# Two-layer cross-attention on one core: scores computed twice, the second time transposed

## The reference

```python
# layer 0: 8 heads of 40; the last 4 context rows are kept apart as "ca"
query, keyt, valt = x @ Wq, enc @ Wk, enc @ Wv              # enc: 371 rows
hs = mha(query, keyt, valt)
ca_q1 = einsum('btc,th->bch', ca, Wq_ca)[:, indices, :]
ca_hs1 = mha(ca_q1, x, x)                                   # the second attention
ca_hs2 = mha(ca_hs1 @ Wq, ca @ Wk_ca, ca @ Wv_ca)           # the third, over 4 keys
x1 = (hs + ca_hs2) @ Wout + b_out + x
# layer 1: 20 heads of 16, over all 375 rows
out = mha(x1 @ Wq, ctx @ Wk, ctx @ Wv) @ Wo + bo + x1
# mha: softmax(q k^T / sqrt(d)) v
```

## Time and profile before

| | us |
|---|---|
| median of 3 runs | 1012.34 (1012.02 to 1013.36) |
| the profiled execution | 1009.08 |
| its span | 1007.4 |
| TensorE matmul busy | 899.3 (89%) |
| VectorE busy | 640.9 (64%) |
| ScalarE busy | 628.6 (62%) |
| GpSimd busy | 272.3 (27%) |
| mean granted TensorE clock | 0.909 |

### The profile page before, as it was taken

How to read it: one execution, slowest core, us unless ns; L and a number is a source line. 1 busy time by engine, 2 the same in 40 slices (tenths; PEclk the granted TensorE clock), 3 DMA queues, 4 the chain that set the end, 5 groups by cost and what they waited for, 6 DMA issues and landing times.

```text
span 1007.4 us, 23258 instructions
## 1 busy us (share of the span) xinstructions
PE 899.3 (89%) x7048; PEld 721.7 (72%) x7048; DVE 640.9 (64%) x1901; ACT 628.6 (62%) x1958; POOL 272.3 (27%) x312
## 2 busy tenths in 40 slices
PE   5678899998989999888989889889998889899987
PEld 4567677777777778677777777677777777777665
DVE  3353758575765857657586667657676576856753
ACT  2354666666766666666677567666666666766643
POOL 4232223232232223223222232322232223220210
PEclk9588999897989989898999989899899989989966
DMA  5443333131333313123232213333131232312000
GB/s 190 133 83 93 59 92 64 54 76 28 99 58 93 65 58 78 34 82 65 91 65 70 59 30 98 59 93 63 52 81 39 81 65 91 65 59 51 15 7 6
DMA packets 49664, 69.06 MB, mean 69 GB/s; under 512 B 10656, under 2 KB 44064, under 8 KB 49552
## 3 DMA queue, kind: packets, MB, share of 16 engines
q1 hardware_dynamic: 48784, 65.30, 27.4%
q0 software_dynamic: 768, 2.29, 0.7%
HBM read 18.93 MB, written 2.42 MB: 21 GB/s over the span
## 4 chain that ended last, share of the span: by engine, by line
PE 73%; ACT 9%; DVE 8%; issue 6%; SPq 2%; DMA 2%; ACTq 0%; POOL 0%; DVEq 0%
PE bankX L868 23%; PE bankT L1003 16%; PE bankO L1028 15%; PE bankS L994 7%; ACT arena L530 4%; ACT arena L647 3%; DVE arena L822 3%; DVE negmax L764 3%; PE bankS L987 2%; PE bankX L929 2%; SPq L387 2%; PE bankX L977 1%; PE bankX L970 1%; PE bankX L950 1%; DMA k_stack<-stage 1%
## 5 line engine op out<-in xcount | busy, mean ns | idle before, releaser
L764 DVE TENSOR_REDUCE negmax<-bankS 112x1 f32<-112x375 f32 (+1 forms) x448 | 241.6, 540 | 228.6 <-PE bankS L994 177.6
L647 ACT ACTIVATE arena<-bankS,negmax 112x375 f32<-112x375 f32 (+1 forms) x448 | 255.8, 571 | 54.9 <-DVE negmax L764 47.6
L639 ACT ACTIVATE arena<-bankT 125x336 f32<-125x336 f32 x320 | 143.5, 449 | 165.7 <-PE bankT L1003 165.7
L1003 PE MATMUL bankT<-cst,arena 112*125 112x112 f32 x1344 | 215.6, 300 | 0.1
L1003 PEld LDWEIGHTS bankT<-cst,arena 112*125 112x125 f32 x1344 | 182.2, 204 | 33.7 <-issue 33.2
L1028 PE MATMUL bankO<-arena,v 125*32 125x112 f32 (+1 forms) x2688 | 188.5, 279 | 0.0
L822 DVE TENSOR_SCALAR arena<-arena,rsum 112x375 f32<-112x375 f32 (+1 forms) x352 | 176.1, 500 | 2.5
L1028 PEld LDWEIGHTS bankO<-arena,v 125*32 125x32 f32 (+1 forms) x2688 | 132.8, 125 | 45.0 <-issue 36.0
L437 POOL TENSOR_TENSOR arena<-arena,rsum 112x375 f32<-112x375 f32 x96 | 77.2, 809 | 160.8 <-DVE rsum L769 160.6
L994 PE MATMUL bankS<-k_stack,q1T 48*112 48x376 f32 x320 | 93.4, 452 | 4.1 <-ACT arena L647 3.7
L647 ACT ACTIVATION_READ_ACCUMULATOR arena<-bankS,negmax 112x1 f32 x448 | 91.1, 203 | 0.0
(11 more groups left out here) (113 smaller groups left out, 1445.3 us busy)
## 6 DMA issues: line engine op xcount, KB each, us to landing
k_stack<-stage SPq DMA_DIRECT2D x96, 176.2 KB
k_stack<-stage SPq DMA_DIRECT2D x192, 70.5 KB, 2.5
k_stack<-stage SPq DMA_DIRECT2D x192, 47.0 KB, 2.1
ctx_raw<-in_ctxT SPq DMA_DIRECT2D x16, 376.0 KB, 3.7
k_stack<-stage SPq DMA_DIRECT2D x48, 117.5 KB
xp<-in_xpad SPq DMA_DIRECT2D x16, 224.0 KB, 3.6
x_raw<-in_xT SPq DMA_DIRECT2D x16, 168.0 KB, 2.5
out<-x1b POOLq DMA_DIRECT2D x16, 140.0 KB, 2.3
```

The costliest lines, as they stand in the source:

```text
L639: nc.scalar.activation(probT[0:KC, h % TSLOTS], bankT[h % 2][0:KC, 0:NKC * SQ] .rearrange("p (k q) -> p k q", k=NKC), ACT.Copy)\
L647: nc.scalar.activation(prob[0:SQ, s % PSLOTS, 0:keys], bankS[s % 2][0:SQ, 0:keys], ACT.Exp, bias=negmax[:, s:s + 1], accum_out=psum_[:, s: ...
L764: nc.vector.tensor_reduce(negmax[:, s:s + 1], bankS[s % 2][0:SQ, 0:keys], axis=AX, op=ALU.max, negate=True).then_inc(max_done, 1)
L1003: last = nc.tensor.transpose(bankT[s % 2][0:KC, k * SQ:(k + 1) * SQ], prob[0:SQ, s % PSLOTS, KC * k:KC * k + KC], ident[0:SQ, 0:SQ])
```

## The change

The probabilities are no longer transposed. Heads go in **groups** of four (2 of layer 0, 5 of layer 1), and an iteration has seven **slots**, with one group's scores in each: slots 0 and 1 layer 0 of batch t, slots 2 to 6 layer 1 of batch t - 1. For a group: scores as before, but only for the maximum (VectorE takes two heads in one reduction); the four maxima are transposed to rows on TensorE (`transpose_m`), copied to `mT` by VectorE, and put by DMA, on SP's queue, into one further row of the transposed queries (`place_m`); the key stacks have a row of ones there. Then `shifted_scores` computes the scores a second time, keys as rows, with the maximum subtracted inside the product, into the three banks of bankST; ScalarE takes the exponential of all four heads in one instruction (layer 1) or two (layer 0) straight into the layout that `attend` reads. The values have a column of ones, so attend gives the row sums too. Outputs are transposed back and divided in new units (N0, N1a, N1b), and then transposed for the output projection (hn0T, hn1T). The maxima of a group are transposed one slot after its scores, shifted scores and attend come two slots after.

Further: four heads of layer 1 attend in four column strips in place of two in two; the third attention's products with Wout are computed once for all batches in the prologue (g_rows) and loaded per batch (gst, p3T), so out0 has nine passes in place of twelve; all units of a slot stand in one block between the slot's two pairs of scores; the loop is written out in full; SP issues the output stores in place of GpSimd.

```diff
-LAG_T, LAG_PV = 4, 6
...
+SLOTS, LAG, GROUP = 7, 2, 4
...
+UNITS = [
+    ([("W2", 1), ("K1_0", 0), ("K1_1", 0), ("q1T_0", -1)], []),
+    ([("q1T_1", -1), ("q1T_2", -1), ("q0", 1), ("N1a", -2), ("p3T", 0), ("K1_2", 0)], []),
+    ([("V1_0", 0), ("N1b", -2), ("V1_1", 0), ("hn1T", -2), ("V1_2", 0)], []),
+    ([("q0T_0", 1), ("S2_0", 1), ("S2_1", 1), ("out1", -2)], []),
+    ([("N0", 0), ("K0_0", 1), ("K0_1", 1), ("q0T_1", 1), ("T2_0", 1)], []),
+    ([("hn0T", 0), ("T2_1", 1), ("K0_2", 1), ("out0", 0), ("PV2", 1)], []),
+    ([("x1T", 0), ("V0_0", 1), ("S3", 1), ("V0_1", 1), ("q1", 0), ("V0_2", 1)], []),
+]
...
+SCORED = {}
+for t in range(B + 1):
+    for i in range(SLOTS):
+        if i < SLOT_L1 and t < B:
+            SCORED[t, i] = (0, t, i)
+        elif i >= SLOT_L1 and t >= 1:
+            SCORED[t, i] = (1, t - 1, i - SLOT_L1)
...
+            def place_m(g):
+                layer, b, k = g
+                n = NUMBER[g]
+                src = mT[:, n % MT_BUFS, :].bitcast(F32)
+                sp.wait_ge(mT_copied, n + 1)
+                if layer == 0:
+                    sp.dma_start(q0T[M_ROW0:M_ROW0 + 1, GROUP * k:GROUP * k + GROUP, :].bitcast(F32),
+                                 src.unsqueeze(1)).then_inc(m0_placed, 16)
+                else:
+                    for odd in range(2):
+                        row = 64 * odd + M_ROW1
+                        sp.dma_start(q1T[b % 2][row:row + 1, 2 * k:2 * k + 2, :].bitcast(F32),
+                                     src[2 * odd:2 * odd + 2].unsqueeze(1)).then_inc(m1_placed, 16)
...
+            for t in ITERATIONS:
+                for i in range(SLOTS):
+                    if scored_at(t, i, 1):
+                        place_m(scored_at(t, i, 1))
+                    if i == 0 and t + 1 < B:
+                        load_ctx(t + 1)
+                        load_xp(t + 1)
...
+                    if i == 2 and t < B:
+                        stack_k1(t)
+                    if i == 4 and 0 <= t - 2:
+                        sp.wait_ge(bank_drained[bank("out1", t - 2)], drained("out1", t - 2))
+                        sp.dma_start(out[t - 2], x1b[t % 2][:, :]).then_inc(out_stored[t % 2], 16)
+                    if i == 5 and t + 2 < B:
+                        load_x(t + 2)
+                    if i == 6 and t + 1 < B:
+                        stack_k0(t + 1)
...
+            def exps(g):
+                layer, b, k = g
+                n = NUMBER[g]
+                dst = PT[:, n % 2]
+                act.wait_ge(st_done, n + 1)
+                if n >= 2:
+                    act.wait_ge(pv_done, n - 1)
+                if layer == 0:
+                    nc.scalar.activation(dst[0:KC, 0:2, :], bankST[0:KC, 0:2, 0:GROUP * SQ], ACT.Exp)
+                    nc.scalar.activation(dst[0:KC - NTOK, 2, :], bankST[0:KC - NTOK, 2, 0:GROUP * SQ], ACT.Exp)\
+                        .then_inc(exp_done, 1)
+                else:
...
+            def maximum(g, pair):
+                layer, b, k = g
+                n = NUMBER[g]
+                keys = SKE if layer == 0 else SK
+                first, step = (2 * pair, 1) if layer == 0 else (pair, 2)
+                dve.wait_ge(scores_done, 2 * n + pair + 1)
+                nc.vector.tensor_reduce(negmax[:, n % 2, first:first + step + 1:step], bankS[0:SQ, :, 0:keys], axis=AX,
+                                        op=ALU.max, negate=True).then_inc(max_done, 1)
+
+            def copy_mT(g):
+                n = NUMBER[g]
+                dve.wait_ge(mT_done, n + 1)
+                nc.vector.tensor_copy(mT[:, n % MT_BUFS, :], bank_mT).then_inc(mT_copied, 1)
...
-            def transposes(it, s):
-                pe.wait_ge(prob_ready[s % PSLOTS], it.slot_heads(s))
-                if it.head_at[s] >= 2:
-                    pe.wait_ge(probT_copied[s % 2], it.bank_heads(s, -1))
-                for k in range(NKC):
-                    last = nc.tensor.transpose(bankT[s % 2][0:KC, k * SQ:(k + 1) * SQ],
-                                               prob[0:SQ, s % PSLOTS, KC * k:KC * k + KC], ident[0:SQ, 0:SQ])
-                last.then_inc(probT_done, 1)
...
+                    pe.wait_ge(o_copied, attended)
+                nc.tensor.transpose(bank_mT, negmax[:, n % 2, :], ident[0:SQ, 0:SQ]).then_inc(mT_done, 1)
...
+            def shifted_scores(g):
+                layer, b, k = g
+                n = NUMBER[g]
+                if layer == 0:
+                    pe.wait_ge(m0_placed, 16 * (G0 * b + k + 1))
+                else:
+                    pe.wait_ge(m1_placed, 32 * (G1 * b + k + 1))
+                if n > 0:
+                    pe.wait_ge(exp_done, n)
+                if layer == 0:
+                    for j, h in enumerate(heads_of(g)):
+                        for c in range(NKC):
+                            keys = KC if c < 2 else KC - NTOK
+                            n_bank, col = st_place(layer, j, c)
+                            last = nc.tensor.matmul(bankST[0:keys, n_bank, col:col + SQ],
+                                                    k0_stack[0:M_ROW0 + 1, h, KC * c:KC * c + keys],
+                                                    q0T[0:M_ROW0 + 1, h, :], start=True, stop=True)
+                else:
+                    for even_c, odd_c in ((2, 0), (0, 1), (1, 2)):
+                        for pair in range(2):
+                            for odd, c in ((0, even_c), (1, odd_c)):
+                                if odd == 1 and c == 2 and pair == 0:
+                                    pe.wait_ge(even_done, G1 * b + k + 1)
+                                j = 2 * pair + odd
+                                h = GROUP * k + j
+                                row = slice(64 * odd, 64 * odd + M_ROW1 + 1)
+                                n_bank, col = st_place(layer, j, c)
+                                last = nc.tensor.matmul(bankST[0:KC, n_bank, col:col + SQ],
+                                                        k1_stack[b % 2][row, h // 2, KC * c:KC * c + KC],
+                                                        q1T[b % 2][row, h // 2, :], start=True, stop=True)
+                                if odd == 0 and c == 2 and pair == 1:
+                                    last.then_inc(even_done, 1)
+                last.then_inc(st_done, 1)
+
...
+                if layer == 0:
+                    at_once = [(c, j) for pair in range(2) for c in range(NKC) for j in (2 * pair, 2 * pair + 1)]
+                else:
+                    at_once = [(c, j) for c in range(NKC) for j in range(GROUP)]
...
+                        v = v0[0:keys, c, 64 * h:64 * h + 64]
+                    else:
+                        keys = KC
+                        at = (2 + n % 2) * SQ
+                        dst = bankO[32 * j:32 * j + 32, at:at + SQ]
+                        v = v1[b % 2][0:keys, c, 32 * h:32 * h + 32]
+                    n_bank, col = st_place(layer, j, c)
+                    last = nc.tensor.matmul(dst, v, src[0:keys, n_bank, col:col + SQ], start=(c == 0),
+                                            stop=(c == NKC - 1))
...
-            def iteration(it):
-                for s in range(0, HEADS, 2):
...
-                    if it.head(s):
-                        scores(it, s)
-                        scores(it, s + 1)
-                    if it.head(s - LAG_T):
-                        at, h = it.head(s - LAG_T)
-                        transposes(at, h)
-                        transposes(at, h + 1)
-                    for at, u in it.units(s) + it.units(s + 1):
-                        unit(at, u)
-                    if it.head(s - LAG_PV):
-                        attend(*it.head(s - LAG_PV))
...
+            for t in ITERATIONS:
+                for i in range(SLOTS):
+                    g, before, late = scored_at(t, i), scored_at(t, i, 1), scored_at(t, i, LAG)
+                    if g:
+                        scores(g, 0)
+                    if late:
+                        shifted_scores(late)
+                    if before:
+                        transpose_m(before, NUMBER[late] if late else attended)
+                        transposed = NUMBER[before] + 1
+                    for u in units_of(t, i, 0):
+                        unit(*u)
+                    if g:
+                        scores(g, 1)
+                    if late:
+                        attend(late, transposed)
+                        attended = NUMBER[late] + 1
+                    for u in units_of(t, i, 1):
+                        unit(*u)
```

1209 lines of the change are left out of this document (647 added, 562 removed).

## The result

| | before | after |
|---|---|---|
| median of 4 runs, us | 1012.18 (1004.97 to 1013.36) | 1233.25 (1230.84 to 1246.04) |
| the profiled execution; its span | 1009.08; 1007.4 | 1246.04; 1244.3 |
| TensorE, VectorE, ScalarE busy, us | 899.3, 640.9, 628.6 | 951.1, 462.0, 402.2 |
| mean granted TensorE clock | 0.909 | 0.766 |

The ratio is 1.222, 95% interval 1.214 to 1.231: slower by 22%. The forecast was 1160 in a range of 1050 to 1250.

A forecast was written before the change was run, and what follows sets the result against it. TensorE was taken to set the pace, 58.3 us a batch. Prologue 60, first iteration 43, fourteen batches of 69 (966) and the rest 87 gave a span of 1156, forecast 1160; own range 1110 to 1200, wide range 1050 to 1250.

The forecast's parts named there:

- D: Rival: shifted-score matmuls of 112 columns cost 0.23 us each, 5.5 more a batch; 1198 up to 1240 us; chance 0.14.
- E: Rival: the clock stays low for most of a batch, costing 14 us each; 1282 us; chance 0.08.
- Two stalls by SP's queue: Shifted scores in slot 4 wait 5.0 us for maxima behind k1_stack; slot 0's scores wait 3.4 for k0_stack.
- Unit prices: TensorE, ScalarE and VectorE times per operation from the earlier profile, such as 0.75 us for six transposes of a head pair.
- Part 1: TensorE's work in a batch: about 45 us where before it was 48, shifted scores priced like transposes.
- Part 2: ScalarE and VectorE lose most work; bank waits behind the 1.3 us exponential, walked slot by slot, make 55.5 a batch.
- Rival C: Bank waits inside the blocks vanish because ScalarE drains at once, clock full: 57.6 a batch, 998 us; chance 0.10.
- Part 3: SP's queue: maxima and stack copies delay each other, stalls of 5.0 and 3.4 us, period 64.0.
- Part 4: Half clock after each of the two long stalls: 2.5 us each, 5 a batch, bounds 0 and 14, period 69.
- The bound of 14: Upper bound, in us a batch, on the half-clock cost; 5 was taken.
- Rival B: The clock holds because transposes leave and real matmuls come, so no half-clock cost: 1088 us; chance 0.20.
- The rest: Stretch after the fourteen batches, the last one and the drain: 87 us, before 94.7.

The follow-up runs named there:

- e1: Changed kernel with k1_stack's 24 DMAs issued in pieces of nine, nine and six in slots 2 to 4: 1129.6 us profiled, other runs 1147.5 to 1182.4.
- e2: Changed kernel with unit K0_2 moved from slot 5 to 4 and k0_stack's nine DMAs issued in slot 5, not 6: 1147.3 us, ratio 1.132.
- e3: Changed kernel with the edits of e1 and e2 together: 1080.7 us, ratio 1.067.
- e12: Changed kernel with the maxima placed from ScalarE's queue in place of SP's, stack copies left on SP: 1139.0 us, ratio 1.122.
- e11: e8 with units reordered, stack copies spread over slots 1 to 5, and batch 1's x loaded and split ahead of the g_rows stores' waits: 853.7 us, ratio 0.840.
- e8: e3 with each slot's units in two places, between the pairs of scores and behind attend, in place of one block: 952.1 us, ratio 0.943.
- e5: Changed kernel with useless matmuls filling both stalls, 32 before layer 1's first shifted scores and 18 before a batch's first scores: 1212.5 us, ratio 1.197.
- e5b: e5 with 21 useless matmuls in place of 32 ahead of layer 1's first shifted scores: 1226.5 us, ratio 1.213.
- e10: Changed kernel with the load of batch 1's x ahead of the twelve g_rows stores in SP's queue: one execution, 1237.2 us.

## Why the prediction was right, and where its sum was short

**How right.** The direction and the wide range hold; the forecast's own range (1110 to 1200) does not. The 1233 is 73 above the 1160 and 17 inside the upper bound. Of the rivals near it, D (1198 to 1240) had a cause that is refuted below, and E (1282) had the clock low for most of a batch, where it came to 0.79.

**Right: what decides.** Two stalls by SP's queue, once a batch each, at the two places named; the waits at the third unit of a block; half clock behind. e1 and e2 took one stall away each, e3 both, e12 the common cause.

**Unit prices and Part 1.** A shifted group took 1.35 for layer 0 (576.88 to 578.23; taken: 1.4) and, at full clock, 0.73 to 0.83 for layer 1 (taken: 0.85); an attend of four strips 0.78 (median of 80; taken: 0.75), one of layer 0 1.31 (1.4). The transposes' price for an unseen form held within 4% for layer 0 and was up to 14% high for layer 1. TensorE's work was put at about 45. The five terms written there add up to 46.0; the walk of Part 2, slots less waits, has 44.9; in e11, at a clock of 0.99, TensorE is busy for 607.4 / 14 = 43.4. Rival D, a price of 0.23 a matmul, is out: twelve took 1.35.

Per head, four strips cost 0.195 and two 0.33, so four are 1.7 times as fast as two. The Trainium skill, page "TensorEngine Tiling (Array Packing)", section "Theoretical Speedup", has up to 4 times for 32 columns and up to 2 times for 64, twice as much for the one as for the other; measured is 1.7.

**Part 2.** The exponential took 1.29 (1.3) and the double maximum 0.93 (0.90):

```profile
L736 DVE TENSOR_REDUCE negmax<-bankS 112x2 f32<-112x750 f32 (+1 forms) x224 | 208.7, 932 | 120.1 <-PE bankS L1095 64.8
L548 ACT ACTIVATE arena<-bankST 125x1344 f32<-125x1344 f32 x80 | 103.4, 1292 | 308.2 <-PE bankST L1137 308.2
```

The waits I had walked are there: q0 1.05 (1.0), p3T 0.88 (0.75), the maximum after slot 1 0.93 (0.85), S2_1 1.20 (0.9), K0_2 1.61 (1.35). Slots at full clock: 6.5, 9.7, 7.8 and 8.2 for 0, 1, 2 and 5 in e1 to e3 against 6.3, 9.4, 7.5 and 8.4. Two slots are off, with half clock in part of each: slot 3 (9.6 against 8.1) and slot 6 (10.2 in e2 and e3 against 8.85). In the changed kernel both lie behind SP. With SP out of the way they show: e3's period is 61.1 where the walk without stalls has 55.5. Rival C, in which these waits vanish, needed what e8 did by hand.

**Part 3, right in kind, short in size.** Slot 4's shifted scores came 21.7 after slot 2's start (21.0), slot 0's scores 13.8 after slot 6's (12.3). The terms, as medians of the fourteen batches: the 24 copies begin 3.0 after slot 2's start and not 2.4, since the issue of place_m ahead of them, 0.58 in the rows above, had no term, and they took 16.2 (15.87). The nine begin 2.9 after slot 6's start and not 2.3, since a pair of maxima takes SP 1.2 to 1.3, where I had 0.6 from ca_raw's 0.32; they took 8.2 (8.18), and k0_stack was in 2.7 after the last issue ended, where I had 1.8. Together 2.2 a batch, 31 in all. The stalls themselves came to 2.8 and 3.6, where I had 5.0 and 3.4: slots 2 and 3 took 19.0 in place of 15.6, half clock in them, and so TensorE came to the first stall late. The queue hides that, as Part 4 said of these slots.

**Part 4, close in size, in part by luck.** Outside SP's stretches slot 0 lost 2.7 (9.2 against 6.5 in e2), slot 4's rest 1.4 (7.9 behind the landing, against 6.5) and slot 5 1.4 (9.65 against 8.2 in e1): 5.5, where 5 was taken. But the 5 was to be the price of the two stalls, and theirs is 4.1 (e5 put it at about 4). Slot 5's half clock stands behind its own wait of 1.61, and e3, with no stall left, still has it (9.2); Part 4 gave such waits no price. The bound of 14 isn't refuted: in e5b's last batches the clock costs 6.5 more than in its first nine, and no run shows why.

Rival B, a clock that holds because the transposes leave, is out for this kernel: the batches have 0.79, and the last stretch, without transposes of probabilities, 0.61 where before had 0.81. What the transposes cost the kernel before isn't shown: e11, with its 0.99, has neither them nor the waits.

**The sum.** Per batch 64.0 + 2.2 of queue + 5.5 of clock makes 71.7 of the 72.6; the other 0.9 is spread over the walk. Against the 1156 of span: prologue +4 (its clock was 0.65, 0.78 before), first iteration +12, batches +50, the rest +22; together 88. The first iteration I had taken "as before": it waited 11.0 for the x of batch 1, whose load stands behind the twelve stores of g_rows, a queue position that the diff shows and the sum did not visit. Behind it stood a second cause, GpSimd's own wait for the stores ahead of the split of x, as e10 showed and e11 removed. The rest (87) had no working but "a little under before"; it holds a last stall of 7.4 for the maxima and ran at 0.61. In e11, without both, it took 88.8. All four misses have one sign, and each holds a queue or a clock carried over from the kernel before.

## What to carry to other kernels

When a change puts a small, urgent DMA into a queue that also issues bulk copies, walk that queue in order and add up issue times, not bytes: here 24 copies with no hurry kept back two DMAs of 0.9 KB, nine more were issued so late that the next batch waited 3.6 for them, and moving the copies in the queue was worth 152 us of 1233. When producers go through two buffers in turn, look at what their consumer does first in each block: moving one drain ahead of 1.3 us in ScalarE's list was worth 63 us. And judge a restructuring only with its order repaired: the same change is 22% slower or 16% faster than the kernel before, with the same matmuls.

## What was new about the hardware

- A DMA of two rows of 112 numbers (0.9 KB) occupies SP for 0.56 (median of 160 in after), a copy of 16 x 3 x 376 (70 KB) for 0.59, and the load of x (168 KB) for 0.36: here the time of an issue doesn't follow the bytes.
- Waits of at most 1.6 us, several a batch, kept the granted clock at 0.86 (e3_both); with waits of 0.9 and less inside the batches but for one of 2.9, 3.5 a batch in all, it was 0.99 (e11_k1_early).
- In one execution nine batches took 66.3 to 72.2 us and the next five 75.1 each (e5b_fill_21), with 20.5 us in a row at half clock in these, TensorE busy for 18.5 of them. The cause is open.
